# Mamba-2 block of a two-layer model: gate applied after the turn to channels, skip term on ScalarE, work of tile 0 moved ahead of the scan

## The reference

```python
proj = hidden_states @ in_proj_w.T          # gate 512 | x 512, B 128, C 128 | dt 64
conv = conv_b + sum((conv_w[:, i] * xp[:, i:i + l, :] for i in range(K)))   # K = 4, along tokens
xBC = jax.nn.silu(conv)
dt = softplus(dt + dt_bias); A = -exp(A_log)
y = _ssd(x * dt[..., None], dt * A, Bm, Cm)   # chunks of 32 tokens, 64 heads of 8, state 128
y = y + D[None, None, :, None] * x            # the skip term
hg = y * jax.nn.silu(gate)                    # the gate
var = jnp.mean(hg * hg, axis=-1, keepdims=True)
return (hg * jax.lax.rsqrt(var + EPS) * norm_w) @ out_proj_w.T
```

## Time and profile before

| | |
|---|---|
| time, median of 3 runs | 648.99 us (648.83 to 649.03) |
| the profiled execution's own time | 644.79 us |
| its span | 642.9 us |
| mean granted TensorE clock | 0.910 of full speed |
| busy share of the span | PE 79%, DVE 65%, ACT 58%, POOL 23% |
| convolution stage, first tap to last | 300.87 to 328.61 us |
| scan loop, from the segment sums behind tile 0 to the table load on ScalarE after tile 7 | 349.63 to 434 us |
| expert stage | from about 464 us |

### The profile page before, as it was taken

One profiled execution on the slowest core, in us unless ns is written; L12 is line 12 of the kernel. 1 busy time (PEld: TensorE's weight loads), 2 busy tenths in 40 slices (PEclk: granted clock), 3 DMA queues, 4 the chain that ended last, 5 costly groups with the idle time before them and its releaser, 6 DMA issues.

```text
span 642.9 us, 14120 instructions
## 1 busy us (share of the span) xinstructions
PE 511.0 (79%) x5748; PEld 375.8 (58%) x5748; DVE 418.6 (65%) x629; ACT 369.9 (58%) x810; POOL 149.9 (23%) x115
## 2 busy tenths in 40 slices
PE   0287898877687765579979999996499999999980
PEld 0154565755466732354654565576499999995560
DVE  7989989999996678988985867758411111112224
ACT  7996888887898318557677666683512222222212
POOL 1000000000010137712218777320203222222110
PEclk9995599697977989899998999997799999999995
DMA  8700000000010000000000000000699999889816
GB/s 331 232 1 1 1 2 1 2 1 1 2 34 2 1 0 2 1 1 2 2 3 3 3 3 2 3 5 33 203 410 418 422 395 328 330 314 333 341 58 204
DMA packets 18191, 71.16 MB, mean 111 GB/s; under 512 B 4688, under 2 KB 9552, under 8 KB 14544
## 3 DMA queue, kind: packets, MB, share of 16 engines
q1 hardware_dynamic: 14976, 63.97, 26.1%
q0 software_dynamic: 1920, 5.25, 2.4%
q10 hardware_dynamic: 1232, 1.06, 0.5%
HBM read 65.55 MB, written 4.72 MB: 109 GB/s over the span
## 4 chain that ended last, share of the span: by engine, by line
PE 48%; DVE 35%; ACT 10%; issue 4%; DMA 2%; POOL 1%; DVEq 0%; ACTq 0%; POOLq 0%
PE PS L1524 29%; DVE arena L984 4%; DVE arena L1245 4%; DVE arena L977 4%; DVE nmx L1080 3%; PE PS L2058 2%; PE PS L1859 2%; PE PS L2127 2%; PE PS L1608 2%; PE PS L1589 1%; ACT arena L622 1%; PE PS L1876 1%; DVE arena L999 1%; DVE R L1006 1%; DVE arena L998 1%
## 5 line engine op out<-in xcount | busy, mean ns | idle before, releaser
L1524 PE MATMUL PS<-arena 128*128 128x128 f32 (+5 forms) x1360 | 147.0, 286 | 16.9 <-DVE arena L1180 11.5
L1524 PEld LDWEIGHTS PS<-arena 128*128 128x128 f32 (+3 forms) x1360 | 122.6, 162 | 40.8 <-issue 24.2
L622 ACT ACTIVATE arena<-PS,nmx 128x128 f32<-128x128 f32 (+1 forms) x128 | 52.3, 431 | 23.7 <-DVE nmx L1080 23.7
L1472 DVE TENSOR_TENSOR R<-arena,PS 128x128 f32<-128x128 f32 x16 | 4.6, 288 | 87.7 <-ACT arena L894 87.7
L489 POOL DMA_INDIRECT ypair<-arena,oid x20 | 19.8, 988 | 122.1 <-ACT arena L900 122.1
L392 POOL TENSOR_SCALAR arena<-ident,gcol 128x128 f32<-128x128 f32 x4 | 3.5, 890 | 187.6 <-DMA gcol<-in_gcol 187.6
L1589 PE MATMUL PS<-arena 32*128 32x128 f32 (+1 forms) x128 | 24.5, 467 | 28.0 <-ACT arena L622 28.0
L1524 PE MATMUL PS<-arena,R 128*128 128x256 f32 x192 | 44.2, 380 | 0.6 <-ACT arena L900 0.6
L454 POOL TENSOR_TENSOR arena<-arena 128x1024 f32<-128x1024 f32 x16 | 37.6, 2368 | 21.9 <-DVE arena L1293 21.9
L1524 PEld LDWEIGHTS PS<-arena,R 128*128 128x128 f32 x192 | 35.2, 190 | 5.1 <-issue 1.0
L984 DVE TENSOR_TENSOR_SCAN arena<-dmat,arena 128x1023 f32<-128x1023 f32 x16 | 37.6, 2348 | 0.6
(11 more groups left out here) (318 smaller groups left out, 1174.9 us busy)
## 6 DMA issues: line engine op xcount, KB each, us to landing
arena<-in_moe SPq DMA_DIRECT2D x23, 1408.0 KB, 8.0
arena<-in_moe SPq DMA_DIRECT2D x23, 768.0 KB, 9.3
inproj<-in_inproj SPq DMA_DIRECT2D x1, 1344.0 KB, 10.4
arena<-in_fT SPq DMA_DIRECT2D x2, 512.0 KB, 4.2
R<-in_w1T SPq DMA_DIRECT2D x1, 1024.0 KB, 6.6
R<-in_w2T SPq DMA_DIRECT2D x1, 1024.0 KB, 8.6
R<-in_w3T SPq DMA_DIRECT2D x1, 1024.0 KB, 10.6
xT<-in_xT SPq DMA_DIRECT2D x1, 1024.0 KB, 12.6
```

The costliest lines, as they stand in the source:

```text
L622: sc.activation(pr[u % 2][:, j, 0:n], PS[:, 2 * (u % 2) + j // 2, (j % 2) * 256:(j % 2) * 256 + n], ACT.Exp, bias=nmx[:, u % 2, j:j + 1], ...
L1524: last = mm(dst, l, r, start=(n == 0), stop=(n == len(pairs) - 1))
```

## The change

1. `gate_in` makes the gate with channels on the partitions: 2 matmuls of 512 columns instead of 64 small ones, eight units (4 channel blocks by 2 halves of tokens) instead of eight tiles.
2. The skip term leaves TensorE: `within` loses its 32 matmuls, and ScalarE scales x by D in place (`skipped`, 4 instructions a tile), after x has been turned to tokens. The diagonal matrices that GpSimd made for it are gone.
3. `gated` no longer multiplies by the gate. A new `gated_turn` on VectorE adds the scaled x to the turned tile in PSUM and multiplies by the gate into `hgT`. ScalarE's `turned` keeps only the square, now of `hgT`.
4. On TensorE `turn(i-1)` goes ahead of `within(i)`.
5. Segment sums, exponentials, the turn of B and the masked decays of tile 0 are put among convolution blocks 3 to 5, the turn of x between gates 4 and 5; GpSimd makes `steps` of tiles 0 to 2 at once (tile 1 in a region of its own). Convolution block 3 is split around the first segment sums. In the loop, `within(0)` goes ahead of the states of tile 0, and `steps(i+2)` behind `masked_decay(i)`.
6. Four small memsets on VectorE move from behind the convolution to before `gate(2, 1)`; `gate_step(7, 6)` moves behind `weighted(0)`, and its numerator is kept in `R`, so that the exponentials of tile 0 have a place.

```diff
@@ gpsimd
+                if i == 3:
+                    pool.wait_ge(S["pe_gate"], NT)
+                pool.tensor_tensor(steps_of(i), dAq[:, i].rearrange("p c j n -> p (c j n)").unsqueeze(2).broadcast_to([P, SH, Q]),
...
-            pool.wait_ge(S["dve_scan"], 16)
-            for k in range(XT):
-                last = pool.tensor_scalar(diag[:, k, :], ident[:], dskip[:, k:k + 1], None, ALU.mult)
-            last.then_inc(S["pool_made"], 1)
             pool.wait_ge(S["dve_dt"], 3)
             pool.wait_ge(S["dve_num"], 8)
-            steps(0)
-            pool.wait_ge(S["pe_gate"], NT)
-            steps(1)
+            for i in range(3):
+                steps(i)
             masked_decay(0, 0)
             masked_decay(0, 1)
-            for i in range(NT - 1):
+            for i in range(1, NT):
+                masked_decay(i, 0)
+                masked_decay(i, 1)
                 if i + 2 < NT:
                     steps(i + 2)
-                masked_decay(i + 1, 0)
-                masked_decay(i + 1, 1)
@@ scalar
+            conv_start(2)
+            act.wait_ge(S["dve_num"], 8)
+            decays(0, 0)
+            decays(0, 1)
+            conv_start(3)
+            decays(0, 2)
+            decays(0, 3)
+            conv_silu(0)
+            conv_start(4)
+            conv_silu(1)
+            conv_silu(2)
+            gate_silu(0)
+            conv_silu(3)
+            conv_start(5)
+            out_weights(0)
+            out_weights(1)
+            gate_silu(1)
+            conv_silu(4)
+            gate_silu(2)
+            out_weights(2)
+            out_weights(3)
+            gate_silu(3)
+            conv_silu(5)
+            gate_silu(4)
+            gate_silu(5)
+            by_chunk(0)
+            gate_silu(6)
+            gate_silu(7)
+            sc.preload_act_table_set(LN_EXP)
...
+                act.wait_ge(S["dve_hgt"], i + 1)
...
+                sc.activation(sqT[i % 2], hgT[i % 2], ACT.Square).then_inc(S["act_sqt"], 1)
+
+            def skipped(i):
+
+                act.wait_ge(S["pe_tok"], 2 * i + 1 if i else 2)
+                for l in range(XT):
+                    x = xc[:, l, i * P:(i + 1) * P]
+                    last = sc.activation(x, x, ACT.Copy, scale=dskip[:, l:l + 1])
+                last.then_inc(S["act_skip"], 1)
...
                 if i + 1 < NT:
                     by_chunk(i + 1)
+                skipped(i)
                 if i:
                     turned(i - 1)
@@ vector
             for n in range(6):
+                if n == 5:
+                    tok_b(0)
...
             gate_step(7, 5)
-            gate_step(7, 6)
...
-                    done(v.tensor_tensor(u[:, :, 1:, :], u[:, :, 1:, :], yd[:, :, 1:, :], ALU.add))
-                    done(v.tensor_tensor(h4[:, :, 0, :], yd[:, :, 0, :], g[:, :, 0, :], ALU.mult))
-                    done(v.tensor_tensor(h4[:, :, 1:, :], u[:, :, 1:, :], g[:, :, 1:, :], ALU.mult), "dve_hg")
+                    done(v.tensor_copy(h4[:, :, 0, :], yd[:, :, 0, :]))
+                    done(v.tensor_tensor(h4[:, :, 1:, :], u[:, :, 1:, :], yd[:, :, 1:, :], ALU.add), "dve_hg")
...
-                    done(v.tensor_tensor(vt, vt, bank(6), ALU.add))
                     done(v.tensor_tensor(vv4[:, :, 1:, :], vv4[:, :, 1:, :], u[:, :, 1:, :], ALU.add))
-                    done(v.tensor_tensor(h4, vv4, g, ALU.mult), "dve_hg")
+                    done(v.tensor_tensor(h4, vv4, yd, ALU.add), "dve_hg")
+
+            def gated_turn(i):
+
+                dve.wait_ge(S["pe_t"], i + 1)
+                dve.wait_ge(S["act_skip"], i + 1)
...
+                y = bank(2).rearrange("p (c l t) -> p l c t", c=NC, l=XT)
+                x, g = (w.rearrange("p l (c t) -> p l c t", c=NC) for w in (xc[:, 0:XT, tile], sg[:, :, tile]))
+                done(v.tensor_tensor(y, y, x, ALU.add))
+                done(v.tensor_tensor(hgT[i % 2].rearrange("p (l c t) -> p l c t", l=XT, c=NC), y, g, ALU.mult), "dve_hgt")
...
+            front_x(0)
+            weighted(0, (3, 4))
+            gate_step(7, 6)
...
                 if i + 1 < NT:
                     front_b(i + 1)
+                if i:
+                    gated_turn(i - 1)
@@ tensor
-                o = bank(1 - i % 2).rearrange("p (h c q) -> p h c q", h=16, c=NC)
-                for c in range(NC):
-                    for kt in range(CT):
-                        for l in range(XT):
-                            last = mm(o[column(l), :, c, :], A[:, kt, chunk_of(i, c)], inproj[:, kt, l * P:(l + 1) * P],
-                                      start=(kt == 0), stop=(kt == CT - 1))
-                last.then_inc(S["pe_gate"], 1)
+                ch, l = divmod(i, XT)
+                acc(bank(1 - i % 2), [(inproj[:, kt, l * P:(l + 1) * P], A[:, kt, ch * HALF:(ch + 1) * HALF]) for kt in range(CT)], "pe_gate")
...
+            pe.wait_ge(S["dve_cv"], 1)
+            conv_half(3, 0)
+            segments(0, 0)
+            conv_half(3, 1)
+            segments(0, 1)
+            pe.wait_ge(S["dve_cv"], 2)
+            conv_in(4)
+            gate_in(0)
+            pe.wait_ge(S["dve_cv"], 3)
+            conv_in(5)
+            tokens_b(0)
+            for i in range(1, 5):
+                gate_in(i)
+            tokens_x(0)
+            for i in range(5, NT):
+                gate_in(i)
...
-                for c in range(NC):
-                    for l in range(XT):
-                        mm(o[column(l), :, c, :], xc[:, l, chunk_of(i, c)], diag[:, l, :], start=(c == 0), stop=False)
...
-                within(i)
                 if i:
                     turn(i - 1)
+                if i:
+                    within(i)
                 between(i)
```

More of the change, by code:

```diff
@@ L771, in decays @@
                     .then_inc(S["act_seg"], 1)
-            def state(i, c):
-                act.wait_ge(S["pe_s"], SBEF[i] + max(c, 2))
-                if i and c == 1:
-                    act.wait_ge(S["pe_yo"], i)
-                sc.activation(sst[:, c - 1, :], bank(4 + (c - 1) % 2), ACT.Copy).then_inc(S["act_s"], 1)
             def by_chunk(i):
@@ L788, in by_chunk, with conv_silu, out_weights @@
                 last.then_inc(S["act_xbd"], 1)
+            def conv_silu(n):
+                act.wait_ge(S["dve_cv"], n + 1)
+                k = XBC_ORDER[n]
+                sc.activation(xc[:, k, :], xc[:, k, :], ACT.Silu).then_inc(S["act_xc"], 1)
+            def out_weights(k):
+                sc.activation(outproj[:, k, :], outproj[:, k, :], ACT.Copy, scale=normw[:, k:k + 1]).then_inc(S["act_opw"], 1)
+            conv_start(0)
+            conv_start(1)
+            for n in range(NC + 2):
+                decay_exp(n)
@@ new lines, in _, with state @@
+            out_weights(2)
[8 more added lines that the diff above has]
+            sc.preload_act_table_set(LN_EXP)
+            def state(i, c):
+                act.wait_ge(S["pe_s"], SBEF[i] + max(c, 2))
+                if i and c == 1:
+                    act.wait_ge(S["pe_yo"], i)
+                sc.activation(sst[:, c - 1, :], bank(4 + (c - 1) % 2), ACT.Copy).then_inc(S["act_s"], 1)
@@ L790, in turned @@
             def turned(i):
-                act.wait_ge(S["pe_t"], i + 1)
+                act.wait_ge(S["dve_hgt"], i + 1)
                 if i >= 2:
                     act.wait_ge(S["pe_op"], i - 1)
-                src = bank(2).rearrange("p (c l t) -> p l c t", c=NC, l=XT)
-                turns = [(hgT, ACT.Copy), (sqT, ACT.Square)]
-                for w, fn in turns if i < NT - 2 else turns[::-1] if i == NT - 2 else turns:
-                    sc.activation(w[i % 2].rearrange("p (l c t) -> p l c t", l=XT, c=NC), src, fn).then_inc(S["act_hgt"], 1)
+                sc.activation(sqT[i % 2], hgT[i % 2], ACT.Square).then_inc(S["act_sqt"], 1)
@@ L808, in _ @@
             act.wait_ge(S["dve_R"], 8)
-            for q in range(4):
-                decays(0, q)
-            by_chunk(0)
             for i in range(NT):
@@ L1223, in _ @@
                     scan_forward(7, 2)
+            for w in (xw[0][96:128, 0, :], xw[1][96:128, 0, :], btok0[0][96:128, :], btok0[1][96:128, :]):
+                done(v.memset(w, 0.0))
             gate(2, 1)
@@ L1364, in _ @@
             add_out(NT - 2)
+            gated_turn(NT - 1)
             gate_tiles(1)
@@ L1818, in _ @@
                 decay_sum(n)
[L1819 to L1826 removed]
             def tokens_x(i):
+                if i == 0:
+                    pe.wait_ge(S["act_xc"], 6)
                 if 1 <= i <= 2:
@@ L1941, in mean_square @@
                 acc(PS[:, 3, 0:P], [(ones[:], sq1[i % 2])], "pe_op")
-            pe.wait_ge(S["act_xc"], 6)
-            tokens_x(0)
-            tokens_b(0)
-            for j in range(2):
-                segments(0, j)
             for i in range(NT):
+                if i == 0:
+                    first_states(i)
                 if i + 1 < NT:
```

99 lines of the change are left out of this document (40 added, 59 removed).

## The result

The changed kernel takes 651.89 us (median of 16 runs, 648.98 to 654.66) where the kernel before, on the same chips, takes 645.32 (16 runs, 642.78 to 649.03). The ratio is 1.0084, 95% interval 1.0063 to 1.0105: 5.4 us slower (the two medians by themselves are 6.6 apart). The likeliest case of the forecast, no change, did not come. The two profiled executions are 652.37 and 644.79 us.

The account below looks back on a forecast made before the run. TensorE was taken to bound the scan loop, with TensorE and VectorE both nearly full in the convolution stage. Terms +1.4 +0.5 -2.0 +0.1 -0.9 +0.1 +0.6 +0.2 summed to 0.0: 649.0 us, no change, range 646.5 to 652.3.

Parts of the forecast that it names:

- Part 1: Convolution stage: memsets moved into VectorE's 1.25 us wait take 1.65, so the gate and all behind it start 0.4 later.
- Part 2: Convolution block 3: TensorE stops 6.2 us for GpSimd's `steps(0)`; the early segment sums bring only 0.4 us by tile 0's end.
- part 3: Behind the stop in block 3: TensorE's clock falls to half speed, losing 1.8 us; tile 0 ends +1.4 against before.
- Part 4: Tile 1: ScalarE holds up the second segment sums, 10.2 us against 9.66, +0.5.
- Part 5: Tile 2: TensorE no longer held by VectorE, 11.0 us against 12.98, -2.0.
- Part 6: Tiles 3 and 5: `turn` waits for VectorE to read bank 2, using up the 0.88 saved; +0.1 each.
- Part 7: Tile 4: no such wait for VectorE, -0.9 us; `gated_turn` ends 0.3 before the output product needs it.
- Part 8: Tiles 6, 7 and the end: ScalarE sets the pace in tile 6, +0.6; the last `gated_turn` at the end, +0.2.
- The stop is cheap: Rival, convolution stage: GpSimd ends sooner or the clock stays up, 646.7 us; chance 0.17.
- The convolution chain takes over: Rival, convolution stage: late block 3 leaves ScalarE and VectorE no slack, 2 us on top, 651.0; chance 0.33 including longer low clock.
- The skip stays cheap everywhere: Rival, scan loop: ScalarE is not late in tiles 1 and 7, 1.1 us less, 647.9; chance 0.10.

Follow-up runs that it names:

- experiment 1: Changed kernel plus three extra gate products, results unused, in TensorE's 6.07 us stop ahead of the first segment sums: ratio 1.0012 to the kernel before.
- experiment 5: Changed kernel with `within` in two halves of 8 heads and three unused gate products in TensorE's stop: ratio 1.0016 to the kernel before.
- experiment 8: Kernel before plus 32 unused 32x32 matmuls (128 instructions) ahead of a TensorE wait near 212 us: ratio 1.0077 to the kernel before.
- experiment 3: Changed kernel plus 32 unused 32x32 products (128 instructions) in TensorE's stop: ratio 1.0009 to the kernel before.
- experiment 4: Changed kernel with `within` of tiles 1 to 7 in two halves, the first 8 heads ahead of the third state: ratio 1.0012 to the kernel before.
- experiment 2: Changed kernel with convolution blocks 3 and 4 ahead of the first segment sums, ScalarE's order following: ratio 1.0068 to the kernel before.
- experiment 6: Changed kernel with `within` in two halves and ScalarE's skip scaling left out (one element scaled a tile): ratio 0.9972 to the kernel before.
- experiment 10: Changed kernel with `within` in two halves, but tile 0's segment sums, turns and exponentials behind the last gate again: ratio 1.0218 to the kernel before.

## Why the prediction was right or wrong, point by point

The range (646.5 to 652.3) holds the 651.89 us, but that is luck. It was laid around a median of three runs of the kernel before, 648.99; 16 runs gave 645.32. Laid around that, the same range is 642.8 to 648.6, and the measured time is 3.3 above it. (The upper end, worked out from its own terms, 651.0 and 1.6, would have been 652.6.) The forecast was no change, and the ratio says 5.4 us slower, more than any rival of the slower side gave. The two errors, of the base and of the change, hid each other.

The terms below are differences between the two profiles; they add up to 4.9 us at the last product into `xT`. The 1.0 us that follows in the routing stage has no counterpart in the ratio that I can show: before has 21.7 us from that product to the first turn of the expert stage, and every other kernel here has 22.2 to 23.3.

- *Part 1, memsets.* +0.4 predicted, +0.6 measured: they took all of VectorE's idle time, and the sums start 0.58 later (301.47 against 300.89).
- *Part 2, the stop.* Right: 6.2 predicted, 6.07 measured, released by GpSimd; block 3 late at VectorE. VectorE had other work until 318.92, not 315.1, as its product was held beside `steps`; it would have waited anyway.
- *Part 3, the clock.* The size was right (2.1 us in experiment 1 for 1.8). But keeping the clock up gains half of that at most, since it then falls in tile 1 (experiment 5). Parts 1 to 3 together: +1.4 predicted, +0.7 measured (350.33 against 349.63).
- *Part 4, tile 1.* 10.2 predicted, 11.18 measured, of which 0.67 is a wait for instructions. ScalarE let TensorE go on 4.6 us into the tile, where 4.4 was predicted; but TensorE was ready at 2.7 and not at 3.7, so it waited 1.87.
- *Part 5, tile 2.* 11.0 predicted, 12.71 measured. Without the 1.52 of waiting for instructions it is 11.19. **This is the step that failed,** here first and again in parts 6 and 8: the sum takes TensorE's time in a tile as its matmuls and its waits for other engines, and puts waits for its own instructions at nothing, without a reason. "TensorE is no longer held and pays what an even tile costs without the skip" was right about VectorE, and another hold came in.
- *Part 6, tiles 3 and 5.* +0.1 each predicted. The turn wait came (0.96 and 0.97). Tile 3 has 1.06 of waiting for instructions besides; without it it is 0.5 over the kernel before, as the work from `turn` to the output product took 3.7 us and not 3.3. Tile 5 (+0.7) has no such wait, but the clock falls: granted 0.65 from 407 to 410 us, behind the turn wait, so `turn` and `within` took 0.96 and 1.94 instead of 0.63 and 1.3. That was not foreseen.
- *Part 7, tile 4.* -0.9 predicted, -1.07 measured.
- *Part 8, tiles 6, 7 and the end.* +0.6 predicted for 6 and 7. Measured: -1.74 and +3.22, and without the waits for instructions (0.80 in tile 6 before, 1.60 in tile 7 after) +0.7. The wait for ScalarE in tile 7 is 2.63 where it was 0.35. The end: +0.2 predicted, +0.3 measured.

In one sum: waits for instructions +3.4 (4.85 against 1.44), all else +1.5 where 0.0 was predicted. Taking the stops out one by one is arithmetic. That waits for instructions can cost this much is shown by experiment 8, where 7.3 us more of them came with 7.1 us more of L and 5.0 by the ratio, and nothing else was touched; that the changed kernel's loss goes with their placing is shown by experiments 3 and 4 (1.0009 and 1.0012), though in both the clock changed somewhere too. Experiment 3 also shows that a stop beside another engine's lateness costs little. The share of 3.4 in the 4.9 us is therefore an estimate.

The rivals. *The stop is cheap* fell with its reasons: GpSimd did not end sooner and the clock did fall. Yet taking the stop out gains only 0.8 us at tile 1 (experiment 2). *The convolution chain takes over* is not so in the changed kernel, where TensorE has no wait behind its stop; it is so once the stop is removed (experiment 2), because VectorE's chain had become 5.2 us longer, 4.3 of it from products beside `steps`. That is why taking the stop out gave so little. *The skip stays cheap everywhere* fell in tile 7 (experiment 6). The cause of the slowdown was in none of them, and the slower side got 0.32 for another reason. The sign could have been hinted at: before already has an unexplained 0.24, 0.40 and 0.80 in the loop, the last of them booked on ScalarE, whose copy had been done; whether the change would make that more or less could not be told without counting instructions.

What stays open: the comparison of both kernels free of waits for instructions; what later `steps` would give the front; and why the clock falls behind a wait of 0.97 us in tile 5 of the changed kernel or in tile 3 of experiment 1, or behind 1.87 us in tile 1 of experiments 1, 5 and 10, and not behind the same waits in the others.

## What to carry to other kernels

When a stretch of hundreds of tiny matmuls shows gaps released by "issue", look at the instruction transfers before blaming the code beside them, and place such a stretch so that larger matmuls cut it. Before believing a change of under 1% in such a kernel, shift its instructions by some with work that nobody needs: here that alone moved an unchanged kernel by 0.8%. Before moving GpSimd's work among VectorE's, look at which of VectorE's products have both inputs in SBUF. And a move into another engine's idle time is worth what that engine has left in the tightest tile: ScalarE had none in tile 7, and the scaling was paid for there.

## What the hardware showed that I had not expected

- TensorE stops 0.2 to 1.8 us at points of its instruction stream that move with the number of instructions ahead of them. Each stop ends 1.2 to 1.5 us behind a packet of 16,384 bytes (0.9 to 1.5 us long) on the instruction queue.
- VectorE's product of two SBUF operands, 0.69 us alone, took 3.67 beside GpSimd's `steps` and ended at 318.92, 0.55 behind it (310.70 + 7.67 = 318.37); with the stop removed (experiment 2) a second one took 1.99 beside the next `steps` and also ended 0.55 behind it. The first step of `gate_step(7, 5)` took 1.96 beside the masked decays instead of the 1.2 its kind takes, 0.7 us for which the prediction had allowed 1.
- VectorE adds into PSUM in place (line 1364, 128x512) in 0.70 us, no more than the 0.69 of the earlier trace rows.
